# Second products of the mixture of experts in pairs: bursts of two experts on TensorE

## The chip, the cores and the metric

The kernel runs on one core of a Trainium2 chip. The core has TensorE (PE; its weight loads are listed as PEld), VectorE (DVE), ScalarE (ACT), GpSimd (POOL) and SyncE (SP), which only issues DMAs here. Each engine works through its own queue in order, and they meet at semaphores. The metric is the time of one execution on the device in microseconds; it is the median of several runs.

## What is computed

Four layers follow each other on x of 8 x 1024 x 256 floats: causal attention, a feed-forward layer with product-key experts, a rotary attention, and a mixture of experts. Only the last is touched by the change. Cut to what matters:

```python
x = x + mixture(layernorm(x))

def mixture(x):                     # D=256, H=8 slices, E=16 experts, K=2, HD=32, I=128
    h = x @ Wm + bm
    t = h.reshape(tokens * H, HD)   # each token has 8 slices of 32 numbers
    w = softmax(t @ expert_emb)     # 16 gates for each slice
    topw, topi = top_k(w, K)
    hmid = gelu(einsum('td,edi->tei', t, W1) + b1)
    eo = einsum('tei,eio->teo', hmid, W2) + b2
    comb = sum(eo[topi] * topw)     # the two chosen experts
    return comb.reshape(tokens, D) @ Wo + bo
```

The kernel works out all 16 experts for every slice and multiplies by a gate that is zero for those not chosen.

## The kernel before

`mixture_ffn` (from line 1942) is the stage. It cuts the tokens into NM = 16 blocks of TM = 512. A block has NU = 32 units: two halves hc of the features (4 slices each) by E = 16 experts. Tokens lie along the free dimension, 512 at a time.

**A unit** u goes through five steps on four engines.
- `hidden` (PE, L2139): the first product, in two pairs p = 0, 1. A pair fills one of HPB = 3 buffers `hidden` in PSUM, of two banks each, with two matmuls of 512 columns (a slice each). Pairs are numbered k = 2u + p within the block, and pair k waits until the gelu of pair k - 3 is done.
- gelu (ACT, L2239): one activation of 128 x 1024 for a pair, into one of four slots of `gelu_out`.
- `expert_out` (PE, L2149): the second product of the unit, 4 slices in 4 column groups of the array, as 8 matmuls in the trace, into the one bank `expert_out`.
- `gate_unit` (DVE, L2336): adds b2 and multiplies by the gates in `gates_spread`, into `gated` (two slots), or, for the first expert of a half, into `combined`.
- `sum_up` (POOL, L2221): adds `gated` to `combined`. At the start of a block the same queue adds the bias row to the block's x tiles (L2210).

**The order on PE** is written out by hand: `hidden(u)`, then `expert_out(u - 1)`, then a piece if the tables give one for that u. Unit 0 of a block waits, besides, for the slices (`slices_in`), and its first pair for the last hidden pair of the block before whose buffer it takes over.

**The front** is the preparation of the next block, cut into pieces and laid between units by `FRONT_AT`: n (normalize two tiles, DVE), x (turn a tile, PE, then a DVE copy), h (project on Wm, PE, then two DVE operations), s (split for the two-part product, DVE), l (gate logits, PE, then a copy), m (maxima, DVE), d (logits less the maximum, and the mask, DVE), the exp on ACT (`EXP_AT`), r (sum and reciprocal, DVE), k (keep the two chosen, DVE, L2307), w (weigh, DVE, L2312), g (turn the gates, PE, L2116, then a copy). `OUTPUT_AT` lays the four outputs of the block before (L2124, with wo) at u = 15, 15, 16 and 17. All PE pieces use the one bank `misc_bank`: each waits (`misc_free`) until DVE has emptied it of the piece before.

**SP** stores the turned gates to DRAM (L2047) and spreads them from there over the partitions, four units at a time (L2057); it also stores and loads the slices of the next block. ACT issues the store of a finished block's output at u = 20.

**POOL's fences**: `let_front_pass` holds an addition back until the DVE piece that lies at the same place (n, s, d, k or w) is done.

Of the kernel before, what the change touches and what calls it, by code (L numbers as in the profile page):

```python
# [1941 lines left out]
def mixture_ffn(nc, X, STATS, MEAN, RS, B, weights, out, ident):  # L1942
# [10 lines left out]
    HPB = 3  # L1953
    GE, GGROUPS = 4, 4
    NG = NU // GE
    with ExitStack() as ctx:
# [3 lines left out]
        def sem(name):  # L1960
# [11 lines left out]
        LS = sb("logits", [P, TT, H, E])  # L1972
        LM = sb("logits_less_max", [P, TT, H, E])
        EX = sb("gate_exp", [P, TT, H, E])
        MK = sb("gate_mask", [P, TT, H, E])
# [8 lines left out]
        OP = ctx.enter_context(nc.psum_tensor("expert_out", [P, TM], F32))  # L1984
        MB = ctx.enter_context(nc.psum_tensor("misc_bank", [P, TM], F32))
# [12 lines left out]
        misc_done = sem("misc_done")  # L1998
        misc_free = sem("misc_free")
        lm_ready = sem("lm_ready")  # L2000
        ex_ready = sem("ex_ready")
        gates_kept = sem("gates_kept")
# [3 lines left out]
        o_done = sem("o_done")  # L2006
        y_ready = sem("y_ready")
# [5 lines left out]

        FRONT = [("n", 0), ("n", 1), ("x", 0), ("x", 1), ("x", 2), ("x", 3), ("h", 0), ("s", 0), ("h", 1), ("s", 1),
                 ("l", 0), ("m", 0), ("m", 1), ("d", 0), ("r", 0), ("k", 0), ("w", 0), ("g", 0)]
        ON_PE = "xhlg"
# [6 lines left out]
        FPB = TT + HC + 2  # L2023

        def before(m):

            return FPB if m == 0 else (FPB + TT) * m + FPB - TT

# [3 lines left out]
        def _(sp):  # L2032
# [12 lines left out]
            def store_gates(m, par):  # L2045
                sp.wait_ge(misc_free, before(m) + 1)
                sp.dma_start(gate_d[par], GTS[:, :]).then_inc(gates_stored, 16)  # L2047
                sp.wait_ge(gates_stored, 16 * (m + 1))

            def spread(m, par, q):  # L2050

                hc, e = divmod(GE * q, E)
                if m or q >= GGROUPS:
                    sp.wait_ge(y_ready, NU * m + GE * (q - GGROUPS + 1) + 1)
# [26 lines left out]
            for t in range(TT):  # L2081
                sp.wait_ge(misc_free, before(NM - 1) + TT + t + 2)
# [4 lines left out]
        def _(pe):  # L2087
            pe.sem_inc(o_done, 2)

            def turn_x(m, t, k):  # L2090
                pe.wait_ge(xn_ready, TT * m + t + 1)
                pe.wait_ge(misc_free, k + 1)
                for c in range(DC):
                    mm = nc.tensor.transpose(MB[:, c * P:(c + 1) * P], XN[:, t, c * P:(c + 1) * P], ident[:, :])  # L2094
                mm.then_inc(misc_done, 1)

            def project(m, h, k):
                pe.wait_ge(misc_free, k + 1)
                for c in range(DC):
                    mm = nc.tensor.matmul(MB[:, :], wm[:, c, h * P:(h + 1) * P], XT[:, c, :],  # L2100
                                          start=(c == 0), stop=(c == DC - 1))
                mm.then_inc(misc_done, 1)

            def logits(m, _, k):
                pe.wait_ge(misc_free, k + 1)
                for t in range(TT):
                    for h in range(HC):
                        mm = nc.tensor.matmul(MB[:, t * P + h * G * E:t * P + (h + 1) * G * E],  # L2108
                                              HX[:, h, t * P:(t + 1) * P], embd[:, :, :], start=True, stop=True)
                mm.then_inc(misc_done, 1)  # L2110

            def turn_gates(m, _, k):
                pe.wait_ge(gates_ready, m + 1)
                pe.wait_ge(misc_free, k + 1)
                for t in range(TT):
                    mm = nc.tensor.transpose(MB[:, t * P:(t + 1) * P], EXP[:, t, :], ident[:, :])  # L2116
                mm.then_inc(misc_done, 1)

            def output(m, par, t, k):
                if t == 0:  # L2120
                    pe.wait_ge(y_added, NU * m + NU + 1)
                pe.wait_ge(misc_free, k + 1)
                for h in range(HC):
                    mm = nc.tensor.matmul(MB[:, 0:D], CM[:, par, h, t * P:(t + 1) * P], wo[:, h, :],  # L2124
                                          start=(h == 0), stop=(h == HC - 1))
                mm.then_inc(misc_done, 1)

            def hidden(m, par, u, first):

                hc, e = divmod(u, E)  # L2130
                for p in range(2):
                    k = 2 * u + p
                    if k >= HPB:
                        pe.wait_ge(gelu_done, NP * m + k - HPB + 1)
                    elif not first:
                        held = next(i for i in range(NP - 1, 0, -1) if i % HPB == k)
                        pe.wait_ge(gelu_done, NP * m - NP + held + 1)
                    for j in range(2):
                        mm = nc.tensor.matmul(HP[k % HPB][:, j, :], w1s[:, e, :], HS[:, par, G * hc + 2 * p + j, :],  # L2139
                                              start=True, stop=True)  # L2140
                    mm.then_inc(a_done, 1)

            def expert_out(m, u):
                hc, e = divmod(u, E)
                n = NU * m + u
                pe.wait_ge(y_ready, n + 1)
                pe.wait_ge(gelu_done, 2 * n + 2)
                for j in range(G):
                    mm = nc.tensor.matmul(OP[HD * j:HD * (j + 1), :], w2[:, e, :],  # L2149
                                          GH[:, (2 * u + j // 2) % 4, j % 2, :], start=True, stop=True,  # L2150
                                          tile_position=(0, HD * j))
                mm.then_inc(o_done, 1)

            front = {"x": turn_x, "h": project, "l": logits, "g": turn_gates}

            def one_block(m, par, first, last):
                k = before(m)
                for u in range(NU):
                    if u % E == 0:
                        pe.wait_ge(slices_in[u // E], 16 * 4 * (m + 1))  # L2160
                    hidden(m, par, u, first)
                    if u >= 1:
                        expert_out(m, u - 1)
                    elif not first:
                        expert_out(m - 1, NU - 1)
                    for t in () if first else OUTPUT_AT.get(u, ()):
                        output(m - 1, 1 - par, t, k)
                        k += 1
                    if u in FRONT_AT and FRONT_AT[u][0] in ON_PE and not last:
                        part, t = FRONT_AT[u]  # L2170
                        front[part](m + 1, t, k)
                        k += 1
                return k

            k = 0
            for part, t in FRONT:
                if part in ON_PE:
                    front[part](0, t, k)
                    k += 1
            for m in range(NM):  # L2180
                k = one_block(m, m % 2, m == 0, m == NM - 1)
            expert_out(NM - 1, NU - 1)
            for t in range(TT):
                output(NM - 1, 1, t, k + t)

        @block.gpsimd
        def _(pool):
            pool.sem_inc(y_added, 1)

            def let_front_pass(m, u):  # L2190

                m, u = (m, u + 1) if u + 1 < NU else (m + 1, 0)
                if m >= NM - 1 or u not in FRONT_AT:
                    return
                part, t = FRONT_AT[u]
                if part == "n":
                    pool.wait_ge(xn_ready, TT * (m + 1) + 2 * t + 2)
                elif part == "s":
                    pool.wait_ge(slices_ready, HC * (m + 1) + t + 1)
                elif part == "d":  # L2200
                    pool.wait_ge(lm_ready, m + 2)
                elif part == "k":
                    pool.wait_ge(gates_kept, m + 2)
                elif part == "w":
                    pool.wait_ge(gates_ready, m + 2)

            def sum_up(m, par):
# [4 lines left out]
                for u in range(NU):  # L2212
                    hc, e = divmod(u, E)
                    n = NU * m + u
                    pool.wait_ge(y_ready, n + 2)
# [3 lines left out]
                    else:  # L2219
                        let_front_pass(m, u)  # L2220
# [7 lines left out]
        def _(act):  # L2228
            def gate_exp(m):
                act.wait_ge(lm_ready, m + 1)  # L2230
                nc.scalar.activation(EX[:, :, :, :], LM[:, :, :, :], ACT.Exp).then_inc(ex_ready, 1)  # L2231

            def one_block(m, first, last):
                for u in range(NU):
                    for p in range(2):
                        k = 2 * u + p
                        act.wait_ge(a_done, NP * m + k + 1)
                        act.wait_ge(o_done, NU * m + u + 1)
                        nc.scalar.activation(GH[:, k % 4, :, :], HP[k % HPB][:, :, :], ACT.Gelu, bias=b1c[:, u % E:u % E + 1])\  # L2239
                           .then_inc(gelu_done, 1)  # L2240
                    if u == EXP_AT and not last:
                        gate_exp(m + 1)
                    if u == OUT_STORE_AT and not first:
# [192 lines left out]
```

## Time and profile before

| | us |
|---|---|
| median of 3 runs | 4373.39 (4366.82 to 4375.27) |
| profiled execution | 4367.08 |
| its span, first to last instruction | 4365.3 |
| mixture stage, from the first hidden matmul | from 3056.9 to the end |

| engine | busy us over the span | share |
|---|---|---|
| PE | 4077.7 | 93% |
| DVE | 2814.8 | 64% |
| ACT | 2660.3 | 61% |
| POOL | 1553.9 | 36% |

Mean granted clock of PE over the whole span: 0.970.

The shares are means over four layers. What counts for the change is the last 1310 us or so, where the page's slices show PE at nine tenths or more in nearly all of them and ACT at eight. How to read on: first the busy times of one block by stretch, then the chain of waits, which names at each moment the work that everything behind it depended on; then, where the chain stays on one engine, the starts of single instructions, since the matmuls overlap at their ends and only the distance from start to start is what PE spends on one.

### The profile page before, as it was taken

To read this page: it belongs to the slowest core of one execution; us is meant where nothing else is said; L and a number is where in the kernel's file an instruction comes from. 1 tells how busy PE (TensorE), PEld (TensorE's weight loads), DVE (VectorE), ACT (ScalarE), POOL (GpSimd) and SP (SyncE) were. 2 spreads that over 40 slices of the span, in tenths; PEclk is the share of its full clock that TensorE was granted. 3 is DMA by queue.
4 is the path that set the end of the run, shared out by engine and by line. 5 is a ranking of instruction groups with operands and counts; after the bars stand their busy time and mean duration, and the time that the engine had idled before them with its cause. 6 is when DMAs were issued, how large, how long until landed. Compare 5 with 4: busy or idle time off the path is not lost. (4 is left out here: it accounts for less than half of the span.)

```text
span 4365.3 us, 65491 instructions
## 1 busy us (share of the span) xinstructions
PE 4077.7 (93%) x23476; PEld 2382.0 (55%) x23476; DVE 2814.8 (64%) x5635; ACT 2660.3 (61%) x3262; POOL 1553.9 (36%) x1303
## 2 busy tenths in 40 slices
PE   7999899999996899999999989997899999999999
PEld 4444444444444778788787765554344444444443
DVE  6777777777665887878787844554455555554553
ACT  2555555555565554545455524443788889888888
POOL 3122122222223453534344411120445545545545
PEclk7999999999997999999999999999999999999999
DMA  7334234333413324232323230000767666676663
GB/s 179 87 87 102 65 88 101 87 87 80 105 29 105 84 58 114 61 106 69 97 77 90 85 76 1 1 1 23 166 152 162 141 161 161 140 161 153 148 162 90
DMA packets 205762, 429.97 MB, mean 98 GB/s; under 512 B 47585, under 2 KB 72561, under 8 KB 189057
## 3 DMA queue, kind: packets, MB, share of 16 engines
q1 hardware_dynamic: 193360, 411.56, 39.0%
q0 software_dynamic: 4160, 6.35, 0.7%
q10 hardware_dynamic: 7920, 7.87, 0.6%
q8 instruction: 191, 3.13, 0.3%
q14 instruction: 131, 1.07, 0.1%
HBM read 338.59 MB, written 87.03 MB: 98 GB/s over the span
## 5 line engine op out<-in xcount | busy, mean ns | idle before, releaser
L2239 ACT ACTIVATE gelu_out<-hidden,b_col 128x1024 f32<-128x1024 f32 x1024 | 1084.3, 1112 | 163.0 <-PE hidden L2139 162.3
L705 DVE TENSOR_REDUCE maxima<-front 128x1 f32<-128x512 f32 (+3 forms) x1280 | 738.9, 631 | 223.6 <-PE front L513 129.3
L2221 POOL TENSOR_TENSOR combined<-combined,gated 128x512 f32<-128x512 f32 x480 | 619.5, 1291 | 663.6 <-DVE gated L2336 454.9
L605 ACT ACTIVATE probsT<-scoresT 128x1024 f32<-128x1024 f32 (+3 forms) x768 | 584.6, 811 | 298.0 <-PE scoresT L541 293.6
L1168 POOL TENSOR_TENSOR pair_sums<-sims 128x1024 f32<-128x1024 f32 x256 | 483.3, 1905 | 668.3 <-DVEq L1300 412.5
L2336 DVE SCALAR_TENSOR_TENSOR gated<-expert_out,b_col,gates_spread 128x512 f32<-128x512 f32 x480 | 360.1, 750 | 500.2 <-PE expert_out L2149 294.4
L2139 PE MATMUL hidden<-slice_stack,w_stack 128*128 128x512 f32 x2048 | 626.4, 428 | 15.0 <-ACT gelu_out L2239 15.0
L2149 PE MATMUL expert_out<-gelu_out,w_sb 128*32 128x512 f32 x4096 | 547.0, 606 | 26.1 <-DVE gated L2336 13.5
L2139 PEld LDWEIGHTS hidden<-slice_stack,w_stack 128*128 128x128 f32 x2048 | 351.8, 189 | 370.8 <-ACT gelu_out L2239 281.8
L1096 PE MATMUL dense<-xnT,dense_weights 128*128 128x512 f32 x2304 | 536.3, 394 | 13.7 <-ACT silu_down L1202 9.7
L450 POOL TENSOR_SCALAR_AFFINE_SELECT probsT<-probsT 128x512 f32<-128x512 f32 x256 | 162.5, 635 | 1009.9 <-ACT probsT L605 1009.8
L1096 PEld LDWEIGHTS dense<-xnT,dense_weights 128*128 128x128 f32 x2304 | 434.3, 189 | 113.5 <-ACT silu_down L1202 10.6
L507 PE MATMUL front<-k_stack,q_stack 62*128 62x512 f32 (+3 forms) x1536 | 442.2, 434 | 44.1 <-ACT values L589 14.2
L507 PEld LDWEIGHTS front<-k_stack,q_stack 62*128 62x128 f32 x1536 | 219.8, 195 | 301.1 <-DVE maxima L705 183.7
L1223 ACT ACTIVATE pair_exp<-pair_sums,neg_max 128x1024 f32<-128x1024 f32 x256 | 282.7, 1117 | 144.6 <-DVE expert_weight L1330 141.3
L556 PE MATMUL pv<-probsT,values 128*32 128x512 f32 (+3 forms) x3072 | 341.2, 518 | 1.8 <-POOL probsT L450 1.0
L541 PE MATMUL scoresT<-q_stack,k_stack 64*128 64x512 f32 (+3 forms) x1536 | 312.1, 415 | 25.4 <-ACT probsT L605 22.5
L1319 DVE SCALAR_TENSOR_TENSOR pair_exp<-pair_sums,top_pairs,pair_exp 128x1024 f32<-128x1024 f32 x256 | 322.4, 1281 | 10.7 <-ACT pair_exp L1223 10.7
L1330 DVE SCALAR_TENSOR_TENSOR expert_weight<-pair_exp,recip_z,expert_weight 128x1024 f32<-128x1024 f32 x192 | 246.5, 1284 | 8.4
L1133 PE MATMUL dense<-up_sb,silu_down 128*128 128x256 f32 x1024 | 231.8, 379 | 5.1 <-DVE silu_down L1351 5.1
L1127 PE MATMUL dense<-wd_sb,hiddenT 128*128 128x256 f32 x1024 | 236.0, 384 | 0.0
L541 PEld LDWEIGHTS scoresT<-q_stack,k_stack 64*128 64x128 f32 x1536 | 153.1, 192 | 143.7 <-ACT probsT L605 82.3
(205 smaller groups left out, 5124.5 us busy)
## 6 DMA issues: line engine op xcount, KB each, us to landing
gates_spread<-gate_scratch SPq DMA_DIRECT2D x512, 256.0 KB, 4.8
dense_weights<-dense_scratch SPq DMA_DIRECT2D x384, 256.0 KB, 2.8
stack_scratch<-split_parts SPq DMA_DIRECT2D x192, 256.0 KB, 3.1
slice_stack<-slice_scratch SPq DMA_DIRECT2D x128, 256.0 KB, 7.8
q_stack<-stack_scratch SPq DMA_DIRECT2D x64, 384.0 KB, 6.2
k_stack<-stack_scratch SPq DMA_DIRECT2D x64, 384.0 KB, 9.4
slice_scratch<-slice_parts SPq DMA_DIRECT2D x32, 512.0 KB, 6.1
out_x<-x_tiles ACTq DMA_DIRECT2D x15, 512.0 KB, 5.0
```

Source lines behind the costliest of these rows:

```text
L507: mm = nc.tensor.matmul(F[k % 3][:, a * w:at], QS[rows, hf, q, qt * P:(qt + 1) * P], KS[rows, hf, q, kc * BANK:kc * BANK + w], start=True, ...
L541: mm = nc.tensor.matmul(bank[:, e, at:BANK], KS[rows, hf, q, kt * P:(kt + 1) * P], QS[rows, hf, q, c * BANK + at:(c + 1) * BANK], start=Tr ...
L556: mm = nc.tensor.matmul(PV[32 * j:32 * (j + 1), at:BANK], V[:, n % 2, kt, (G * g + j) * HV:(G * g + j) * HV + 32], PT[:, i % NPT, j, at:BA ...
L605: nc.scalar.activation(PT[:, i % NPT, 2 * pr:2 * pr + 2, at:BANK], ST[pr][:, :, at:BANK], ACT.Exp, scale=SCALE).then_inc(probs_ready, 1)
L705: nc.vector.tensor_reduce(dst, F[k % 3][:, 0:parts * w].rearrange("p (a k) -> p a k", a=parts), AX.X, ALU.max)\
L1096: mm = nc.tensor.matmul(bank[:, :], DW[:, u % SLOTS, a, c, :], XT[:, m % 2, b, c, :], start=(c + i == 0), stop=(c == DC - 1 and i == 2))
L1168: nc.gpsimd.tensor_tensor(A[:, h, :].rearrange("p (i j) -> p i j", i=NR), SM[:, m % 2, t, 0, h, 0:NR].unsqueeze(2).to_broadcast([P, NR, NK ...
L2139: mm = nc.tensor.matmul(HP[k % HPB][:, j, :], w1s[:, e, :], HS[:, par, G * hc + 2 * p + j, :], start=True, stop=True)
L2149: mm = nc.tensor.matmul(OP[HD * j:HD * (j + 1), :], w2[:, e, :], GH[:, (2 * u + j // 2) % 4, j % 2, :], start=True, stop=True, tile_positi ...
L2221: nc.gpsimd.tensor_tensor(CM[:, par, hc, :], CM[:, par, hc, :], Y[:, u % 2, :], ALU.add)\
L2239: nc.scalar.activation(GH[:, k % 4, :, :], HP[k % HPB][:, :, :], ACT.Gelu, bias=b1c[:, u % E:u % E + 1])\
L2336: nc.vector.scalar_tensor_tensor(out=Y[:, u % 2, :] if e else CM[:, par, hc, :], in0=OP[:, :], scalar=b2c[:, e:e + 1], in1=GS[:, q % GGROU ...
```

## The change

The stage's order is written in bursts. A burst b takes the units 2b and 2b + 1: first the PE pieces that the table gives for it, then the four hidden pairs of both units, then the second products of units 2b - 1 and 2b. DVE follows the same order: what the PE pieces need of it, then `gate_unit` of both units, then the pieces that are DVE's alone. The numbers b run through all blocks (ALL = 256 bursts), and so do the hidden pairs and their buffers.

The banks `expert_out` and `misc_bank` become `out_bank0` and `out_bank1`, used in turn by second products and pieces alike. The list `USES` numbers these uses in their order; use i waits until DVE has freed use i - 2. `gelu_out` has six slots (GHB) instead of four, and a gelu of unit n waits for the second product of unit n - 3. To make room, the gate work of DVE shares its tiles with `xn` and `xnT`, so that n is now made for the block after the next, in bursts 14 and 15; the maxima come in three parts. POOL's fence for k is gone.

In bursts of a block: x 0 to 3, h and s 4 and 5, l 6, m 6 to 8, d 9, exp behind burst 10, outputs 0 to 2 of the block before in burst 11, output 3 and r in 12, k and w in 13 (and the output's store), g at the head of 14.

```diff
+    GHB = 6
+    BU = NU // 2
+    ALL = NM * BU
...
-        GH = sb("gelu_out", [I, 4, 2, TM])
+        GH = sb("gelu_out", [I, GHB, 2, TM])
...
-        OP = ctx.enter_context(nc.psum_tensor("expert_out", [P, TM], F32))
-        MB = ctx.enter_context(nc.psum_tensor("misc_bank", [P, TM], F32))
+        OB = [ctx.enter_context(nc.psum_tensor(f"out_bank{i}", [P, TM], F32)) for i in range(2)]
...
-        FRONT_AT = dict(zip((0, 1, 2, 3, 4, 5, 6, 7, 8, 9, 10, 11, 12, 13, 18, 19, 20, 22), FRONT))
-        EXP_AT = 14
-        OUTPUT_AT = {15: (0, 1), 16: (2,), 17: (3,)}
-        OUT_STORE_AT = 20
+        FRONT_AT = {0: [("x", 0)], 1: [("x", 1)], 2: [("x", 2)], 3: [("x", 3)], 4: [("h", 0), ("s", 0)],
+                    5: [("h", 1), ("s", 1)], 6: [("l", 0), ("m", 0)], 7: [("m", 1)], 8: [("m", 2)], 9: [("d", 0)],
+                    11: [("o", 0), ("o", 1), ("o", 2)], 12: [("o", 3), ("r", 0)], 13: [("k", 0), ("w", 0)],
+                    14: [("g", 0), ("n", 0)], 15: [("n", 1)]}
+        EXP_AT = 10
+        OUT_STORE_AT = 13
...
+        def outs(b):
+            return [("e", n, 0) for n in (2 * b - 1, 2 * b) if 0 <= n < NM * NU]
...
+            def take(*use):
+
+                if USE[use] >= 2:
+                    pe.wait_ge(bank_free, USE[use] - 1)
+                return bank(*use)
...
+            def hidden(n, p):
+
+                m, (hc, e) = n // NU, divmod(n % NU, E)
+                if (e, p) == (0, 0):
+                    pe.wait_ge(slices_in[hc], 16 * 4 * (m + 1))
+                k = 2 * n + p
+                if k >= HPB:
+                    pe.wait_ge(gelu_done, k - HPB + 1)
...
+            def expert_out(n):
                 pe.wait_ge(gelu_done, 2 * n + 2)
+                ob = take("e", n, 0)
...
+            for b in range(ALL):
+                for part, m, t in fronts(b, True):
+                    front[part](m, t)
+                hidden(2 * b, 0)
+                hidden(2 * b, 1)
+                hidden(2 * b + 1, 0)
+                hidden(2 * b + 1, 1)
+                for _, n, _ in outs(b):
+                    expert_out(n)
...
+            def gelu(n, p):
+                k = 2 * n + p
+                act.wait_ge(a_done, k + 1)
+                if n >= GHB // 2:
+                    act.wait_ge(bank_done, USE["e", n - GHB // 2, 0] + 1)
...
+            for b in range(ALL):
+                for part, m, t in fronts(b, True):
+                    front[part](m, t)
+                for _, n, _ in outs(b):
+                    gate_unit(n)
+                for part, m, t in fronts(b, False):
+                    front[part](m, t)
```

`turn_gates` on PE still begins with its wait for `gates_ready`, which w sets on DVE, and `fronts(b, True)` gives the PE pieces of burst b.

## Rows read from the trace of the kernel before

**Rows 1.** Busy time by stretch, a middle block: us, busy (x instructions), granted clock, DMA share, GB/s.
```profile
3566.20:3647.10 80.90, 78.21 (x441) 33.89 (x437) 42.05 (x90) 70.99 (x68) 41.10 (x31) 1.00 0.66 154
```

**Rows 2.** Chain of waits, start us, us, what, in a steady stretch.
```profile
3603.87 1.13 PE hidden L2139 x4
3605.00 0.99 PE expert_out L2149 x8
```

**Rows 3.** Timeline of PE in narrow windows: start us, us, engine line op out<-in xcount.
```profile
3627.01 0.61 PE L2149 MATMUL expert_out<-gelu_out,w_sb 128*32 128x512 f32 x4
3627.55 0.50 PE L2139 MATMUL hidden<-slice_stack,w_stack 128*128 128x512 f32 x1
3627.88 0.63 PE L2139 MATMUL hidden<-slice_stack,w_stack 128*128 128x512 f32 x2
3628.35 0.39 PE L2139 MATMUL hidden<-slice_stack,w_stack 128*128 128x512 f32 x1
3628.68 0.62 PE L2149 MATMUL expert_out<-gelu_out,w_sb 128*32 128x512 f32 x1
```

**Rows 4.** Timeline, PE and POOL: groups behind a wait, an addition and the bias.
```profile
3592.24 1.13 PE L2124 MATMUL misc_bank<-wo_sb,combined 128*128 128x256 f32 x4 [0.58 <-DVE x_tiles L2324]
3628.52 1.28 POOL L2221 TENSOR_TENSOR combined<-combined,gated 128x512 f32<-128x512 f32 x1 [0.84 <-DVE gated L2336]
3635.62 2.38 POOL L2210 TENSOR_TENSOR x_tiles<-x_tiles,bo_rows 128x1024 f32<-128x1024 f32 x1
3639.19 1.06 PE L2149 MATMUL expert_out<-gelu_out,w_sb 128*32 128x512 f32 x8 [0.90 <-DVE gated L2336]
```

**Rows 5.** Timeline of ACT around the exp.
```profile
3589.20 1.28 ACT L2231 ACT_TABLE_LOAD   x1
3592.43 3.13 ACT L2239 ACTIVATE gelu_out<-hidden,b_col 128x1024 f32<-128x1024 f32 x3
```

**Rows 6.** Chain of waits, pieces between units, a hidden group behind one, l a block later.
```profile
3572.22 1.91 PE misc_bank L2100 x4
3578.20 1.93 PE misc_bank L2108 x16
3598.75 1.06 PE misc_bank L2124 x4
3642.55 0.37 PE misc_bank L2094 x2
3642.92 0.93 PE hidden L2139 x4
3659.08 1.93 PE misc_bank L2108 x16
```

**Rows 7.** Border of two blocks: chain of waits, then timelines of PE and ACT.
```profile
3629.33 1.11 ACT gelu_out L2239
...
3630.58 0.71 PE L2139 MATMUL hidden<-slice_stack,w_stack 128*128 128x512 f32 x2 [0.84 <-ACT gelu_out L2239]
...
3631.33 1.11 ACT L2239 ACTIVATE gelu_out<-hidden,b_col 128x1024 f32<-128x1024 f32 x1 [0.89 <-PE hidden L2139]
```

**Rows 8.** Timeline: a gated, and keep, weigh and g in the prologue.
```profile
3629.81 0.75 DVE L2336 SCALAR_TENSOR_TENSOR gated<-expert_out,b_col,gates_spread 128x512 f32<-128x512 f32 x1 [1.37 <-POOL combined L2221]
...
3054.65 0.69 DVE L2307 TENSOR_TENSOR gate_exp<-gate_exp,gate_mask 128x512 f32<-128x512 f32 x1 [0.21 <-issue]
3055.44 0.69 DVE L2312 TENSOR_TENSOR gates<-gate_exp,gate_recip 128x512 f32<-128x512 f32 x1
3056.18 1.12 PE L2116 MATMUL misc_bank<-ident,gates 128*128 128x128 f32 x4 [7.86 <-DVE gates L2312]
```

**Rows 9.** DMA issues of the page: out<-in, queue, op xcount, KB each, us to landing.
```profile
gates_spread<-gate_scratch SPq DMA_DIRECT2D x512, 256.0 KB, 4.8
```

**Rows 10.** End of the kernel: first output in the timeline, then a stretch of 2 us.
```profile
4354.06 1.13 PE L2124 MATMUL misc_bank<-wo_sb,combined 128*128 128x256 f32 x4 [2.21 <-POOL combined L2221]
...
4356.00:4358.00 2.00, 1.58 (x4) 0.75 (x3) 0.38 (x1) 0.00 (x0) 0.00 (x0) 0.52 0.19 66
```

More of the change, by code:

```diff
@@ L2125, in output @@
                                           start=(h == 0), stop=(h == HC - 1))
[L2126 to L2146, printed above, removed]
+                mm.then_inc(bank_done, 1)
+            def hidden(n, p):
[5 more added lines that the diff above has]
+                    pe.wait_ge(gelu_done, k - HPB + 1)
+                for j in range(2):
+                    mm = nc.tensor.matmul(HP[k % HPB][:, j, :], w1s[:, e, :], HS[:, m % 2, G * hc + 2 * p + j, :],
+                                          start=True, stop=True)
+                mm.then_inc(a_done, 1)
@@ L2151, in expert_out @@
                                           tile_position=(0, HD * j))
[L2152 to L2173, printed above, removed]
@@ L2175, in _ @@
-            k = 0
+                mm.then_inc(bank_done, 1)
+            front = {"x": turn_x, "h": project, "l": logits, "g": turn_gates, "o": output}
             for part, t in FRONT:
                 if part in ON_PE:
[L2178 to L2182, printed above, removed]
+                    front[part](0, t)
+            for b in range(ALL):
[7 more added lines that the diff above has]
+                    expert_out(n)
@@ L2183, in _ @@
+            for _, n, _ in outs(ALL):
+                expert_out(n)
             for t in range(TT):
-                output(NM - 1, 1, t, k + t)
+                output(NM - 1, t)
         @block.gpsimd
@@ L2230, in gate_exp @@
                 act.wait_ge(lm_ready, m + 1)
-                nc.scalar.activation(EX[:, :, :, :], LM[:, :, :, :], ACT.Exp).then_inc(ex_ready, 1)
-            def one_block(m, first, last):
-                for u in range(NU):
-                    for p in range(2):
[L2236 to L2243, printed above, removed]
-                        act.wait_ge(misc_free, before(m) + (0 if last else FPB - 1) + TT + 1)
-                        act.dma_start(tiles_out[:, TT * (m - 1):TT * m, :], X[:, TT * (m - 1):TT * m, :])\
-                           .then_inc(stored, 16)
@@ L2248, in _ @@
-            gate_exp(0)
-            for m in range(NM):
-                one_block(m, m == 0, m == NM - 1)
+                nc.scalar.activation(EX, LM, ACT.Exp).then_inc(ex_ready, 1)
+            def gelu(n, p):
[3 more added lines that the diff above has]
+                    act.wait_ge(bank_done, USE["e", n - GHB // 2, 0] + 1)
+                nc.scalar.activation(GH[:, k % GHB, :, :], HP[k % HPB][:, :, :], ACT.Gelu, bias=b1c[:, n % E:n % E + 1])\
+                   .then_inc(gelu_done, 1)
@@ new lines, in store_out @@
+            def store_out(m):
+                act.wait_ge(bank_free, USE["o", m, TT - 1] + 1)
+                act.dma_start(tiles_out[:, TT * m:TT * (m + 1), :], X[:, TT * m:TT * (m + 1), :]).then_inc(stored, 16)
+            gate_exp(0)
+            for b in range(ALL):
+                for n in (2 * b, 2 * b + 1):
+                    for p in range(2):
+                        gelu(n, p)
+                if b % BU == EXP_AT and b // BU + 1 < NM:
+                    gate_exp(b // BU + 1)
+                if b % BU == OUT_STORE_AT and b >= BU:
+                    store_out(b // BU - 1)
@@ L2277, in split, with logits, maxima @@
                   .then_inc(slices_ready, 1)
[L2279 to L2283 removed]
+            def logits(m, _):
+                ob = done("l", m, 0)
+                nc.vector.tensor_copy(flat(LS), ob[:, :].rearrange("p (g e) -> p g e", e=E)).then_inc(bank_free, 1)
+            def maxima(m, part):
                 dve.drain()
[L2285 to L2287 removed]
+                for g in range(*MAXIMA[part]):
+                    nc.vector.max(M8[:, g // H, g % H, :], LS[:, g // H, g % H, :])
@@ L2328, in gate_unit @@
+            def gate_unit(n):
+                m, u = divmod(n, NU)
                 hc, e = divmod(u, E)
[L2329 to L2330 removed]
                 q, i = divmod(u, GE)
+                ob = done("e", n, 0)
                 if i == 0:
```

220 lines of the change are left out of this document (100 added, 120 removed).

## The prediction, made before the changed kernel was run

> **What bounds the kernel now.** Only the mixture stage changes: 16 blocks of 512 tokens, 32 units (experts of a half) each, from 3056.9 us to the end. I read the stretches first. A middle block takes 80.88 us (the piece l starts at 3578.20 and again at 3659.08, [rows 6]), with PE busy for 78.21, ACT for 70.99 and DVE for 42.05 at a granted clock of 1.00 [rows 1]. The chain of waits then says who leads: in the steady part it stays on PE, with hidden (first product) and expert_out (second product) by turns, 1.13 + 0.99 = 2.12 us a unit [rows 2]. Single starts show where these go [rows 3]: expert_out to the first hidden matmul 0.54, first to second 0.33, then 0.235 each, last hidden to expert_out 0.33, the first four expert_out matmuls to the second four 0.45 (a group of eight takes 1.06, [rows 4], a four 0.61). So 2.12 is PE's own pace without a wait, and changing from one form of matmul to the other is dear: about 0.09 + 0.09 + 0.10 per unit over the plain pitches. ACT runs gelus that wait for nothing at 1.04 each or a little less (three in 3.13, [rows 5]), so about 2.05 a unit: close behind, but not the bound.
>
> The pieces laid between units (front of the next block, output of the last) cost PE their own length less some 0.2, as the hidden group behind them shrinks from 1.13 to 0.93 [rows 6]: x 0.37, so 0.17 net; h 1.91, so 1.71; l 1.93, so 1.79 (0.99 behind it); o 1.06, so 0.86; g has four short matmuls where x has two, so 0.4. A block has 4 x, 2 h, 1 l, 1 g, 4 o: 0.7 + 3.4 + 1.8 + 0.4 + 3.4 = 9.7. With 32 x 2.12 = 67.9 that is 77.6; the other 3.3 are stalls. One is at the border of blocks, where hidden 0 shares its bank with the last hidden pair and waits for its gelu: the previous expert_out began at 3628.68, the next hidden was due 0.45 + 0.54 later at 3629.67 and starts at 3630.58, 0.9 late [rows 3, 7]. Another 0.9 is an expert_out that waits for gated through POOL's bias addition, and the second output waits for the one misc bank: its idle is 0.58, behind a matmul that it would have overlapped by some 0.2, so it starts 0.8 late [rows 4]. The remaining 0.5 to 0.7 goes with the exp.
>
> **Bursts (the main term).** The new order on PE is: pieces, hidden pairs 4b, 4b+1, 4b+2, 4b+3, then expert_out 2b-1 and 2b. PE's own time falls: 0.33 + 6 x 0.235 + 0.33 + 3 x 0.45 + 0.54 = 3.96 a burst, where two units took 4.24: 0.28 saved. That expert_out follows expert_out at 0.45 isn't in the trace; its bounds are 0.43 and 0.54 (a change of form), and I take the row of the same form.
>
> But there are still three hidden buffers. Pair 4b+3 needs the one of pair 4b, so it waits for gelu 4b. Until now the wait was old by a unit when it was reached; now PE comes to it 0.33 + 5 x 0.235 = 1.50 after the burst's first matmul. Gelu 4b starts 0.75 after its hidden pair's start in the released case [rows 7], 0.77 with a second matmul at 0.33 in place of 0.31; it takes 1.11, and 0.14 later PE goes on [rows 7]. So pair 4b+3 starts at 2.02, not 1.50. After a wait its second matmul comes at 0.31 (0.71 for two, less the last one's 0.39 to 0.40) [rows 3, 7], expert_out 0.33 behind, at 2.66. Then 3 x 0.45 + 0.54 end the burst at 4.55. Is gelu 4b really started by PE and not held by ACT? Four gelus end at about 0.77 + 4 x 1.04 = 4.9, the next hidden is ready at 4.55 + 0.77 = 5.3: ACT stands idle and the loop closes on itself, at 4.55. Per burst that is 0.31 more than before, and 16 x 4.55 = 72.8 per block, 4.9 to 5.0 more. Expert_out 2b needs gelu 4b+1, done at about 0.77 + 1.01 + 1.11 + 0.14 = 3.03, and starts at 3.11: just covered; if that slips, PE waits there too. The six gelu slots free ACT of an old wait that the trace doesn't show as a cost: nothing.
>
> **Two banks and the pieces.** Each use waits for the use before the last. Gated starts 1.13 after its expert_out [rows 8] and takes 0.75: for 2b-1 that is 3.79 to 4.54, for 2b 4.70 to 5.45. The first piece behind a burst is due at 4.55 and gets its bank at about 4.6: 0.03 to 0.05 in ten bursts, 0.3 to 0.4 a block. Three outputs in a row find theirs (due at 5.55, free at 5.5; due at 6.4, free at 6.3), so the 0.8 goes. The border wait goes (pairs are now counted through), and so does the bias wait: behind gated 31 POOL adds until about 6.0 and biases until 8.4, by 1.28 and 2.38 [rows 4], and the next gated that needs it comes at 9.4. The exp with its table loads takes 3.23 of ACT (3592.43 - 3589.20, [rows 5]); it now lies beside three outputs, 2.6 of PE, and ACT's spare 0.5: 0.1 left. So all 3.3 of stalls go, 0.4 come.
>
> **The gates' turn (the second term).** keep and weigh now stand in burst 13 behind its two gated, and PE's turn g is the first thing of burst 14, ahead of its hidden pairs. Before, a unit lay between them (weigh at u 20, g at u 22). In the prologue keep, weigh and g follow each other without cover: 3054.65, 3055.44, 3056.18, so 1.53 from keep to g [rows 8]. Here keep can start at 5.45 + 0.09 = 5.54, g at 7.07, and PE was due at 4.6: a stall of 2.5 in each of 15 blocks. All hidden pairs of burst 14 are queued behind that wait, and ACT, out of input, with them. Keep also lost its fence against POOL's addition; bounds 2.2 and 3.0. SP's store and spread of the gates follow g later than before: g to the first gated of the next block is some 14 us; copy, store and spread are under 1.5 + 2 x 4.8 = 11.1 (the store counted like a spread, [rows 9]). Covered by 3; if not, PE waits the difference.
>
> **PE's clock.** At the end of the kernel PE stood idle 2.21 before the first output, and the granted clock was 0.52 in 4356 to 4358, that is mostly 1.2 GHz [rows 10]. The stall of 2.5 is as long. How long a drop lasts I can't read here; if it is about as long again as the stall or a little more, PE loses about half of that, less what the wait for gelu 4b hides anyway: 1.2, an estimate. I count 8 drops in 15 stalls, 10 us; bounds 0 and 25.
>
> The Trainium skill (TensorE: Matmul & The Clock Gate, section "A second HAM failure mode: psum-queue depth-cycling") speaks against this change more widely: PE that micro-idles between groups of matmuls while it cycles through PSUM banks can lose its clock again and again. No row here shows that from waits of 0.5; the block's 1.00 with stalls of 0.9 in it speaks against. It is rival C.
>
> **The sum.** Middle block: 72.8 + 9.7 + 0.4 + 0.1 + 2.5 = 85.5, against 80.88: +4.6, times 14 = 64. Last block: no front and no g, +5.0 - 0.8 = +4. Block 0 has no outputs and waits for gates by DMA; +3.5, between 0 and 8. The clock +10. Prologue and last outputs gain from the second bank, by the 0.8 of an output wait at some seven places: -6, between 0 and -10. Together +75. The profiled execution took 4367.08 (span 4365.3), 6.3 below the median of 4373.39. So 4442 for a profiled one, and 4448 as a median.
>
> **Rivals.** A: the sum, 4448. Its own range is 4405 (no clock loss, and 0.24 for a pair's second matmul after a wait, so 0.07 x 256 = 18 less, and more from the ends) to 4495 (expert_out to expert_out at 0.54, +23; clock +25). B: g's stall is covered by something I miss: 37 less and no clock loss, 4401. C: PE's clock falls in the bursts as well. At half clock a burst's own PE time is about 7.5, 3.0 more than 4.55; were that so in a quarter of 256 bursts, +190: 4638. D, the other side: PE gets ahead, and gelu 4b is started by ACT's own pace, so pair 4b+3 finds its buffer free. Then PE's own time bounds: 16 x 3.96 + 9.7 + 0.4 + 2.5 = 76.0 a block, 4.9 less than before, 15 blocks -73, ends -6, clock +5: 4299. It decides at the point where PE's part after the wait plus 0.77 is shorter than ACT's three gelus left: counted from the end of gelu 4b, 0.14 + (4.55 - 2.02) + 0.77 = 3.44 against 3 x 1.04 = 3.12. The reserve is 0.3; two expert_out groups would have to be a sixth shorter than their rows. E: the bursts' change of forms saves more than two units' rows say and pays for the waits: within 0.2%.
>
> **How the numbers follow.** A 0.70, B 0.08, C 0.05, D 0.11, E 0.06. The range 4395 to 4495 holds A and B and nothing of the rest. A measurement of this kernel tells about 0.2% (9 us) from no change. Slower: A, B, C and a little of E, 0.84; same 0.05; faster 0.11.
>
> **What would show it.** Right: some 256 waits of the fourth hidden pair for gelu, 0.5 each; ACT idle 0.4 to 0.5 before the first gelu of each burst; hidden starts 4.55 apart from burst to burst in bursts 7 to 9; 15 waits of g for weigh of 2.5; no wait at block borders; blocks of 85 to 87. Wrong: the fourth pair at 1.50 without a wait (D), g without a wait (B), or a clock well under 1.00 in blocks' middles (C).

## The result and the profile after

The changed kernel takes 4437.6 us (median of 4 runs, 4421.06 to 4446.83) against 4370.1 for the kernel before (4 runs): slower by 67.5 us, a ratio of 1.0153 with a 95% interval of 1.0126 to 1.018. I had said 4448, and slower by 75.

The page first. The span has grown by 71.1 us, while no engine has over 1.3 us more to do: PE is busy for 4065.8 us (before 4077.7), ACT for 2633.9 (2660.3), DVE for 2816.1 (2814.8). What was added is idle time. The columns are busy us, share of the span and instructions, then the costliest group with the idle time before it.

```profile
span 4436.4 us, 65528 instructions
...
PE 4065.8 (92%) x23476; PEld 2414.1 (54%) x23476; DVE 2816.1 (63%) x5635; ACT 2633.9 (59%) x3262; POOL 1555.0 (35%) x1303
...
L2239 ACT ACTIVATE gelu_out<-hidden,b_col 128x1024 f32<-128x1024 f32 x1024 | 1057.5, 1115 | 260.7 <-PE hidden L2158 260.5
```

One middle block, by stretch (same columns as [rows 1]); the granted clock is 1.00 as before. Below it the starts of the piece l in two blocks that follow each other, from the chain of waits: a block is now 85.25 us long.

```profile
3666.20:3751.40 85.20, 77.17 (x439) 35.57 (x437) 42.05 (x91) 69.24 (x68) 41.10 (x32) 1.00 0.64 145
...
3697.70 1.97 PE out_bank L2129 x16
3782.94 1.97 PE out_bank L2129 x16
```

Who waits for whom, from 3100 to 4400 us (us in total, times, longest); the last two rows are of the kernel before, from 3100 to 4300. The third row has no forerunner there.

```profile
ACT gelu_out L2239 <- PE hidden L2158: 239.1, 230, 4.7
PE hidden L2158 <- ACT gelu_out L2239: 72.0, 242, 3.2
PE out_bank L2137 <- DVE gates L2316: 40.5, 15, 3.0
...
ACT gelu_out L2239 <- PE hidden L2139: 140.1, 158, 1.8
PE hidden L2139 <- ACT gelu_out L2239: 15.0, 16, 2.3
```

PE waits 242 times for a gelu in front of a hidden pair, where before it did so 16 times, about once a block. ACT waits 230 times for PE, 239 us in all, where before it was 158 times and 140 us. Each now waits for the other about once a burst. And 15 times, once a block that has a front, the turn of the gates waits for w on DVE, 2.7 us each. (The row of 242 shows only 0.3 us each. In the trace a matmul lasts 0.39 to 0.40 us, though the next can start 0.235 after it, so the first 0.16 of a wait count as busy.)

The chain of waits in a burst without a piece (start us, us, what); [rows 2] and [rows 7] are what answers to it before.

```profile
3617.87 0.68 PE hidden L2158 x2
3618.55 0.02 issue
3618.57 1.12 ACT gelu_out L2239
3619.69 0.04 issue
3619.74 0.73 PE hidden L2158 x2
3620.47 1.85 PE out_bank L2166 x16
3622.33 0.68 PE hidden L2158 x2
```

Before, the chain stayed on PE here. Now it leaves PE in every burst for one whole gelu. The timeline of PE for the same burst gives the starts:

```profile
3617.80 1.67 PE L2158 MATMUL hidden<-slice_stack,w_stack 128*128 128x512 f32 x6
3619.74 0.73 PE L2158 MATMUL hidden<-slice_stack,w_stack 128*128 128x512 f32 x2 [0.27 <-ACT gelu_out L2239]
3620.40 1.92 PE L2166 MATMUL out_bank<-gelu_out,w_sb 128*32 128x512 f32 x16
3622.26 0.97 PE L2158 MATMUL hidden<-slice_stack,w_stack 128*128 128x512 f32 x3
```

The fourth pair starts 1.94 after the first, the burst ends at 4.46; two units took 4.25.

The gates' turn, chain of waits:

```profile
3653.05 0.75 DVE gated L2340
...
3653.89 0.94 DVE xnT L2311
...
3654.91 0.70 DVE gates L2316
3655.61 0.04 issue
3655.66 1.12 PE out_bank L2137 x4
```

The second gated of burst 13, k (its output tile is a part of `xnT` now), w, and only then g; g is the next thing in PE's queue, so PE stands still. k takes 0.94 where it took 0.69 [rows 8], with an addition of POOL beside it. This is so in all 15 blocks (0.39 to 0.40 us of overlap with the addition); in the prologue of the changed kernel, with the same tiles and no addition beside it, k takes 0.69. So it is the company of POOL and not the new tile.

### The profile page after: what moved, and what is told of

It reads as the page before. It is cut to its first block and busy times, and to the rows that moved or that the text cites. A ratio compares the mean times of both kernels' runs of the same rounds, so it can differ in the third digit from the quotient of the medians.

```text
span 4436.4 us, 65528 instructions
## 1 busy us (share of the span) xinstructions
PE 4065.8 (92%) x23476; PEld 2414.1 (54%) x23476; DVE 2816.1 (63%) x5635; ACT 2633.9 (59%) x3262; POOL 1555.0 (35%) x1303
## 5 line engine op out<-in xcount | busy, mean ns | idle before, releaser
L2239 ACT ACTIVATE gelu_out<-hidden,b_col 128x1024 f32<-128x1024 f32 x1024 | 1057.5, 1115 | 260.7 <-PE hidden L2158 260.5
L2340 DVE SCALAR_TENSOR_TENSOR gated<-out_bank,b_col,gates_spread 128x512 f32<-128x512 f32 x480 | 360.2, 750 | 624.1 <-PE out_bank L2166 600.2
L2166 PE MATMUL out_bank<-gelu_out,w_sb 128*32 128x512 f32 x4096 | 496.0, 602 | 3.5 <-DVE combined L2340 3.0
L507 PE MATMUL front<-k_stack,q_stack 62*128 62x512 f32 (+3 forms) x1536 | 441.7, 434 | 46.3 <-ACT values L589 15.8
L2166 PEld LDWEIGHTS out_bank<-gelu_out,w_sb 128*32 128x32 f32 x4096 | 107.3, 109 | 253.4 <-issue 169.9
```

What stands on the lines that cost most here:

```text
L507: mm = nc.tensor.matmul(F[k % 3][:, a * w:at], QS[rows, hf, q, qt * P:(qt + 1) * P], KS[rows, hf, q, kc * BANK:kc * BANK + w], start=True, ...
L2166: mm = nc.tensor.matmul(ob[HD * j:HD * (j + 1), :], w2[:, n % E, :], GH[:, (2 * n + j // 2) % GHB, j % 2, :], start=True, stop=True, tile_ ...
L2239: nc.scalar.activation(GH[:, k % GHB, :, :], HP[k % HPB][:, :, :], ACT.Gelu, bias=b1c[:, n % E:n % E + 1])\
L2340: nc.vector.scalar_tensor_tensor(out=Y[:, u % 2, :] if e else CM[:, m % 2, hc, :], in0=ob[:, :], scalar=b2c[:, e:e + 1], in1=GS[:, q % GGR ...
```

## The experiments

**Theory A**: the loss has two sources, the wait of each burst's fourth hidden pair for its first gelu, and g's wait for w. Both lie on PE's path, and everything else in the change gains. **Rivals**: R1, g's wait only stands in front of the gates' way over DRAM; R2, bursts save what they should and the two shared banks or the pieces' places cost the time; R3, the changes between the two forms of matmul aren't what PE loses, so bursts have nothing to give; R4 is named with the last kernel. The runs were made on several chips, so between chips I compare ratios to the kernel before, or block lengths in the traces.

### The gates' two steps a burst earlier

```diff
-                    11: [("o", 0), ("o", 1), ("o", 2)], 12: [("o", 3), ("r", 0)], 13: [("k", 0), ("w", 0)],
+                    11: [("o", 0), ("o", 1), ("o", 2), ("r", 0)], 12: [("o", 3), ("k", 0), ("w", 0)],
```

> The changed kernel, with r one burst earlier (behind the outputs of burst 11) and k and w in burst 12, so that w is done a whole burst before g is due. Theory A (the loss has two sources, the fourth pair's wait for gelu 4b in 256 bursts, and g's wait for w in 15 blocks at 2.7 us each): only the second goes, -41 us, 4397; bursts without a piece stay at 4.46 us, burst 13 with g behind it falls from 7.6 to about 4.9. Rival R1 (g's wait stands in front of another that ends as late, the gates' way over DRAM to the next block's first unit): g's wait goes and the same 2.7 us come back at the block's border, 4438.

Measured: 4387.4 us, 1.0045 of before (1.003 to 1.006). Against the changed kernel's 4437.6 (another chip) that is 50 less; by the ratios it is 47. The rows of g waiting for w are gone; a middle block went from 85.25 to 82.65 us, the burst up to the one with g from 7.61 to 5.02, and nothing came back at the border. R1 falls. 15 x 2.6 are 39. Another 3 are half clock: in the changed kernel's trace it followed three of the 15 stalls of g (more on this below), here none. The rest I put down to the spread between runs and chips.

### The bursts alone undone

```diff
                 hidden(2 * b, 0)
                 hidden(2 * b, 1)
+                for _, n, _ in outs(b)[:-1]:
+                    expert_out(n)
                 hidden(2 * b + 1, 0)
                 hidden(2 * b + 1, 1)
-                for _, n, _ in outs(b):
-                    expert_out(n)
+                expert_out(2 * b)
```

> The changed kernel with the bursts alone undone: hidden pairs of unit 2b, second product 2b-1, hidden pairs of unit 2b+1, second product 2b; two banks, numbering, tables and g's place stay. Theory A: the wait for gelu 4b is out of the way, the changes of form come back; two units take 4.2 us and not 4.46, so 256 x 0.26 = -67 us, 4371. Rival R2 (bursts save what they should, and the loss lies in the two shared banks and the places of the pieces): two units get longer by the saved changes, 0.28 to 0.38 us, so +70 us or more, 4508.

Measured: 4380.2 us, 1.0017 of before (0.9997 to 1.0037). Two units take 4.25 us again for 4.46, in all bursts without a piece. R2 said slower than the changed kernel; it is faster by some 57. The block became only 3.3 us shorter though (81.9), where 16 x 0.21 = 3.4 and 1.2 at the pieces were to be had (the two kernels with early gates differ by 82.65 - 78.07 = 4.6). Here the clock falls to 0.50 at every one of the 15 stalls of g, from 0.4 before it starts to 0.8 behind. Three of them, each in a window behind g:

```profile
3558.00:3560.00 2.00, 2.00 (x7) 1.72 (x7) 0.69 (x1) 0.18 (x1) 1.20 (x1) 0.50 0.00 0
3640.00:3642.00 2.00, 2.00 (x8) 1.65 (x7) 0.69 (x1) 0.24 (x1) 1.13 (x1) 0.50 0.00 0
3722.00:3724.00 2.00, 2.00 (x8) 1.58 (x6) 0.69 (x1) 0.32 (x1) 1.06 (x1) 0.50 0.00 0
```

### Both

> Both edits of the two runs above. Theory A: the two sources add up, -41 - 67, 4330, below the kernel before by 40 us: what is left are the gains of two banks, counting through and the pieces' places (3.2 us a block were stalls). Rival R2: 4467. Rival R1: 4371.

Measured: 4323.0 us, 0.989 of before (0.9865 to 0.9916). Both sources gone, the kernel is faster than the one before by 45 us. So all that the change brought besides these two is, taken together, a gain of that size; its parts (two shared banks, pairs counted through, places of the pieces, six gelu slots) were not run one by one. A block takes 78.07 us; PE's own 67.9 and 9.7 are 77.6, so of the 3.3 of stalls before 0.5 are left. The chain of waits of this kernel no longer leaves PE:

```profile
3616.36 0.93 PE hidden L2158 x4
3617.29 0.99 PE out_bank L2166 x8
3618.29 1.13 PE hidden L2158 x4
3619.42 0.99 PE out_bank L2166 x8
```

### The pieces in the gap

The bursts stay (r, k and w are early); the PE pieces move from the head of the burst to between its third and fourth pair.

```diff
-                for part, m, t in fronts(b, True):
-                    front[part](m, t)
                 hidden(2 * b, 0)
                 hidden(2 * b, 1)
                 hidden(2 * b + 1, 0)
+                for part, m, t in fronts(b, True):
+                    front[part](m, t)
                 hidden(2 * b + 1, 1)
```

> The changed kernel with r, k and w a burst earlier, and the PE pieces of a burst laid between its third and its fourth hidden pair, where PE waits for gelu 4b. Theory A: in the ten bursts with pieces the piece covers the wait of 0.4 us (x only 0.33 of it) and the bank's wait of 0.15 goes as well: about 5 us a block less than with r, k and w early alone, -75 us against it, 4325. If the fourth pair's wait is not on the path (rival R2): no gain, 4397.

Measured: 4330.5 us, 0.9918 of before (0.9891 to 0.9946); 57 less than with the pieces at the head, on the same chip. Two bursts of this kernel, without a piece and with g, in PE's timeline:

```profile
3596.82 1.67 PE L2158 MATMUL hidden<-slice_stack,w_stack 128*128 128x512 f32 x6
3598.76 0.73 PE L2158 MATMUL hidden<-slice_stack,w_stack 128*128 128x512 f32 x2 [0.27 <-ACT gelu_out L2239]
3599.42 1.92 PE L2166 MATMUL out_bank<-gelu_out,w_sb 128*32 128x512 f32 x16
3601.28 1.66 PE L2158 MATMUL hidden<-slice_stack,w_stack 128*128 128x512 f32 x6
3602.78 0.60 PE L2137 MATMUL out_bank<-ident,gates 128*128 128x128 f32 x4
3603.21 0.72 PE L2158 MATMUL hidden<-slice_stack,w_stack 128*128 128x512 f32 x2
3603.86 1.92 PE L2166 MATMUL out_bank<-gelu_out,w_sb 128*32 128x512 f32 x16
3605.72 1.67 PE L2158 MATMUL hidden<-slice_stack,w_stack 128*128 128x512 f32 x6
```

With g in the gap the fourth pair follows 1.93 after the first, without it 1.94: the piece costs nothing, since the wait was there anyway. I had 75 for this and it gave 57: the block is 3.8 shorter, not 5. Burst by burst, an x gave 0.33, which is all that it costs at the head with its bank's wait in it (1.3 in all where I had 1.9), and l, the last output and g together 2.4 where I had 1.7. But the two h gave only 0.3 where I had 1.1, and the burst with three outputs became 0.3 longer where I had it 0.5 shorter. Why the h and the outputs came short wasn't tried.

### The wait longer by a gelu

```diff
-                    pe.wait_ge(gelu_done, k - HPB + 1)
+                    pe.wait_ge(gelu_done, k - HPB + 2)
```

> The changed kernel with the wait of each hidden pair one gelu stricter (pair k waits for gelu k-2 where it waited for k-3), as if there were two buffers. Theory A: the fourth pair now starts behind gelu 4b+1, that is at 0.77 + 1.01 + 1.11 + 0.05 = 2.94 us after the burst's start and not at 1.94, and all behind it moves with it: a burst without a piece goes from 4.46 to 5.46 us, +256 us in all, 4694. Rival R2 (the buffer wait lies beside ACT's and DVE's own work, the banks set the pace): a burst grows by less than 0.5, below 4566.

Measured: 4692.3 us (one run; the kernel before 4372.4). The bursts without a piece take 5.46 us.

```profile
3617.16 1.20 PE L2158 MATMUL hidden<-slice_stack,w_stack 128*128 128x512 f32 x4
3619.10 0.74 PE L2158 MATMUL hidden<-slice_stack,w_stack 128*128 128x512 f32 x2 [0.74 <-ACT gelu_out L2239]
3620.10 0.73 PE L2158 MATMUL hidden<-slice_stack,w_stack 128*128 128x512 f32 x2 [0.27 <-ACT gelu_out L2239]
3620.76 1.92 PE L2166 MATMUL out_bank<-gelu_out,w_sb 128*32 128x512 f32 x16
3622.62 1.20 PE L2158 MATMUL hidden<-slice_stack,w_stack 128*128 128x512 f32 x4
```

The fourth pair comes at 2.94, the next burst at 5.46. Each microsecond of this wait is a microsecond of the burst; nothing lies beside it. That settles R2 from the other side. (A middle block without half clock grew by 15.8 us, for 16 bursts. At 12 of this run's 15 stalls of g the clock fell to half, which is in the total.)

### Bursts and units with short gelus

To see what bursts would give if the buffer came free in time, both orders (r, k and w early) with a gelu of half the length. The second slice of each pair gets no gelu of its own, and both second products read the first one's: that part of the computation is left out, PE's work is all there.

```diff
-                nc.scalar.activation(GH[:, k % GHB, :, :], HP[k % HPB][:, :, :], ACT.Gelu, bias=b1c[:, n % E:n % E + 1])\
+                nc.scalar.activation(GH[:, k % GHB, 0, :], HP[k % HPB][:, 0, :], ACT.Gelu, bias=b1c[:, n % E:n % E + 1])\
...
-                                          GH[:, (2 * n + j // 2) % GHB, j % 2, :], start=True, stop=True,
+                                          GH[:, (2 * n + j // 2) % GHB, 0, :], start=True, stop=True,
```

> Bursts with r, k and w early, with gelu on the first slice of each pair only (128 x 512), whose result both second products of the pair read; so the second slice's gelu is left out and the output isn't the reference's. PE's work is the same, a gelu takes about 0.69 us for 1.11. Theory A (the saved changes of form are real, and only the buffer's release outweighs them): the fourth pair finds its buffer free at 0.77 + 0.69 + 0.05 = 1.51 us, where PE comes to it anyway; a burst without a piece takes 4.03 us for 4.46, 256 x 0.43 = -110 us against the same kernel with whole gelus, 4277. Rival R3 (bursts save no changes of form worth naming): about 4.25 a burst as unit by unit, 4333.

> The same cut gelu in the order unit by unit with r, k and w early; the second slice's gelu is left out here too. Theory A: this order has no wait for gelu on its path, PE's own pace sets it: two units stay at 4.25 us, 4323 (to 4315, for ACT no longer late behind pieces). Then bursts with short gelus beat it by 40 to 50 us, which is what they save in changes of form. Rival (ACT's pace bounds the unit order too): it falls as the bursts do, to 4280 or below.

Measured, on one chip: bursts 4281.0 us (0.9809, 0.9793 to 0.9826), units 4317.0 us (0.9883, 0.9864 to 0.9903; a block takes 77.8 us, against 78.07 with whole gelus). Bursts without a piece take 4.03 us for 4.46, as expected to the hundredth, and pairs of units stay at 4.25. Here is such a burst, eight hidden matmuls in one row with no wait in them:

```profile
3619.35 2.24 PE L2158 MATMUL hidden<-slice_stack,w_stack 128*128 128x512 f32 x8
3620.12 2.42 ACT L2239 ACTIVATE gelu_out<-hidden,b_col 128x512 f32<-128x512 f32 x4 [1.61 <-PE hidden L2158]
3621.53 1.92 PE L2166 MATMUL out_bank<-gelu_out,w_sb 128*32 128x512 f32 x16
3623.38 0.95 PE L2158 MATMUL hidden<-slice_stack,w_stack 128*128 128x512 f32 x3
```

So the idea of the change is sound: fewer changes of form save 0.22 per two units without a piece. In all it is 36 us where I had 40 to 50. R3 falls. With whole gelus the release of the buffer takes 0.43 a burst and more than eats it.

### Three pairs at a time

As many pairs as there are buffers, then by turns two second products and one (the order of all engines follows from one list of such steps; r, k and w early).

```diff
+        def steps():
...
+            at, made = {-(-4 * b // 3): b for b in range(ALL)}, 0
+            for s in range(2 * NM * NU):
+                upto = min(NM * NU, 3 * (s // 2) + s % 2)
+                pairs = [k for k in range(3 * s, 3 * s + 3) if k < NM * NP]
+                yield at.get(s), pairs, [("e", n, 0) for n in range(made, upto)]
...
```

> With r, k and w early: steps of three hidden pairs, as many as there are buffers, then by turns two second products and one; so three units have two changes of form to and fro where single units have three and bursts 1.5, and no pair meets a buffer in use. Theory A: PE's own time is 3 units = 12 x 0.235 + 6 x 0.43 + 2 x (0.10 + 0.09 + 0.10) = 5.98 us, 1.99 a unit, close to ACT's 2.03, which then bounds the bursts without pieces; a block takes about 32 x 2.03 + 9.7 + 1 = 75.7 us against 78.1 of the unit order with early gates, so -38 us, 4285. If changes of form are not what PE loses (rival R3: PE waits anyway for what ACT and DVE return), the block stays at 78 or above, 4325.

Measured: 4314.2 us, 0.9868 of before (0.9837 to 0.9899): 58 us below the kernel before on its chip, but 29 above what I had expected. It has the lowest ratio of the kernels that compute everything, but its interval overlaps those of units with early gates (0.989) and of gap or units (0.9882), and its middle blocks take 76.6, 77.8 and 79.4 us by turns, 77.9 in the mean, where those take 78.07 and 77.92. So it can't be told from them. Three units without a piece take 6.47 us and not 6.1. PE's timeline says why my "no pair meets a buffer in use" was wrong:

```profile
3643.71 1.92 PE L2177 MATMUL out_bank<-gelu_out,w_sb 128*32 128x512 f32 x16
3645.57 1.67 PE L2169 MATMUL hidden<-slice_stack,w_stack 128*128 128x512 f32 x6
3647.17 1.07 PE L2177 MATMUL out_bank<-gelu_out,w_sb 128*32 128x512 f32 x8
3648.16 1.20 PE L2169 MATMUL hidden<-slice_stack,w_stack 128*128 128x512 f32 x4
3649.52 0.74 PE L2169 MATMUL hidden<-slice_stack,w_stack 128*128 128x512 f32 x2 [0.16 <-ACT gelu_out L2246]
3650.19 1.92 PE L2177 MATMUL out_bank<-gelu_out,w_sb 128*32 128x512 f32 x16
```

Behind the single second product the six hidden matmuls take 2.03 and not 1.60: the third pair of that step waits for the third gelu of the step before. PE comes to that pair 1.60 + 0.99 + 1.03 = 3.6 after the step before began; the third gelu is done after 0.77 + 3 x 1.01 + 0.1 + 0.05 = 3.95, and that is when the pair starts. The three buffers are the bound again, only later.

### Gap or units

A burst with a piece lays it in the gap, one without goes unit by unit (r, k and w early).

```diff
+                pieces = fronts(b, True)
...
+                if not pieces:
+                    for _, n, _ in outs(b)[:-1]:
+                        expert_out(n)
                 hidden(2 * b + 1, 0)
+                for part, m, t in pieces:
+                    front[part](m, t)
                 hidden(2 * b + 1, 1)
+                for _, n, _ in outs(b) if pieces else outs(b)[-1:]:
+                    expert_out(n)
```

> With r, k and w early: bursts that have a piece lay it before the fourth pair (the wait is covered), bursts without one go unit by unit (no wait). Theory A: the six bursts of a block without pieces go from 4.46 to 4.25 us, the others stay as with the pieces in the gap: 78.85 - 1.3 = 77.6 us a block, 4312. Rival R4 (the two orders disturb each other where they meet, since a unit order needs the second products one step earlier): 4330 or more.

Measured: 4320.8 us, 0.9882 of before (0.9854 to 0.991). A block takes 77.92 us for 78.85; the bursts without pieces 4.25, the one behind the exp 7.7 for 7.4. In that stretch the chain of waits stays on ACT, from 3660.3 us through the gelus and the exp to 3681.6, where PE goes on: the shorter bursts leave ACT no time to catch up. R4 falls, though the estimate was 9 us too good. Against units with early gates (0.989) it can't be told apart; their blocks are 78.07 and 77.92.

## Why the prediction was right

Step by step, with a middle block as the measure: 80.88 before, 85.5 said, 85.25 measured.

- **The burst.** Said 4.55, measured 4.46; 16 of them 71.4 for 72.8. The chain of reasoning held at each link: first pair to gelu 0.77, gelu 1.12, fourth pair behind it, ACT idle at each burst's start, the loop closed on itself. Two sizes were off. PE goes on 0.05 after a gelu that it waits for and not 0.14 as at the border in [rows 7], so the fourth pair starts at 1.94 instead of 2.02. And from the first expert_out matmul to the next burst it is 1.86 for 1.89. Both are small, but times 256 they make 23 us. One reading in the chain was wrong: expert_out 2b doesn't start at 3.11, that is the second half of 2b-1's group; by the sum's own steps it is 2.66 + 2 x 0.45 = 3.56. So it was covered by 0.5 and not just covered, and nothing in the sum hung on it.
- **The saved changes of form.** The half-length gelus show them: 4.25 - 4.03 = 0.22 a burst, where I had 0.28. In the trace of those bursts the fourth pair's second matmul still comes 0.34 after its first and not 0.235.
- **The gates' turn.** Said 2.5 with bounds of 2.2 and 3.0, measured 2.7. The difference is k's 0.94 for 0.69, the fence that I had named as a bound. Moving k and w made it go and nothing took its place.
- **The pieces.** Here I was too low. The four x cost 0.33 each and not 0.21, h, h and l together 5.6 for 5.3, the four outputs with the exp 3.9 for 3.6. The first piece's bank was to be late by 0.03 to 0.05; as the burst ends 0.09 earlier than I said, and 0.15 passes from gated's end to x's start, it is 0.2 late. Together about 1.1 us a block, and with g's 0.2 nearly what the shorter bursts gave back (1.4). That the block's total is closer than its terms is luck.
- **The stalls of before.** Border, bias and the second output went, as said. In the unit order with early gates 0.5 of 3.3 is left.
- **The clock.** Said 8 drops at 1.2 us, 10 in all. In the changed kernel the clock fell to 0.50 behind g in three of the 15 blocks: in block 0, and in two middle blocks, which are longer than 85.25 by 1.4 and 0.9. The two stretches below lie at g or just behind it in these two; the middle block by stretch above has the same stall of 2.7 us in it and stayed at 1.00.

```profile
3229.00:3231.00 2.00, 2.00 (x7) 1.62 (x6) 0.69 (x1) 0.60 (x1) 0.78 (x1) 0.50 0.00 0
3655.00:3657.00 2.00, 1.34 (x6) 1.25 (x7) 0.79 (x2) 0.00 (x0) 1.23 (x1) 0.51 0.00 0
```

So 10 us were counted and about 3 came. The price of one was right, the count was a guess. Rival C, the clock falling within the bursts, is out: 1.00 over a whole block, with a wait in every burst. The rule of the Trainium skill that I weighed (TensorE: Matmul & The Clock Gate, "A second HAM failure mode: psum-queue depth-cycling"), by which PE that micro-idles between groups of matmuls while it cycles through PSUM banks can lose its clock again and again, didn't show at waits of half a microsecond.
- **The ends.** Said -6 from prologue and last outputs. The last block with its end took 88.6 us for 87.7, where +4 for its bursts less 3 of these 6 were said. Of the 71.1 us between the profiled executions 67.2 lie behind the first hidden matmul. From the first turned tile to that matmul it took 22.9 for 24.5, but between 21.5 and 24.5 in the other kernels, whose prologue is the same as the changed one's, so the gain that I had counted there isn't shown. The first turned tile itself lies 5.4 us later, behind layers in which nothing was changed; between the other kernels' executions this start differs by more than that.

The middle blocks' 14 x 4.37 = 61, with 3.3 for block 0 (91.6 for 88.3, its half clock included), 2.2 for the clock in the middle blocks and 0.9 for the end make 67.6, and the trace has 67.2. That the medians differ by the same 67.5 is in part chance: the four runs of the changed kernel spread from 4421 to 4447. The forecast of 75 came as near as it did because its errors have both signs: bursts 23 too long, clock 7 too dear, pieces and g some 20 too cheap.

Rival D had its point of decision at 3.44 against 3.12, PE's part behind the wait against ACT's three gelus. Measured, the reserve was about as said: ACT was idle before the first gelu of every burst, 0.3 us in the bursts without a piece.

## What to carry to other kernels

Grouping like instructions to save changes of form lengthens the time between two uses of the same buffer; before counting the saving, walk once around the ring: first producer, consumer, release, and the producer that needs the buffer again. If that way is longer than the group, the engine can wait once per group, as here. Two remedies gained here over bursts with early gates: a smaller group (three pairs for three buffers, which still waited 0.3 us in every second step without a piece) and other work laid in front of the instruction that waits. Neither did measurably better than no groups at all. And a piece that another engine must finish first belongs a step away from it: the same k, w and g cost nothing or 2.7 us a block by their place alone.

## What was not expected of the hardware

- A stall of PE is followed by the half clock in some blocks or in all, and the stall's length doesn't decide it. In the changed kernel PE stood idle for 2.7 us at g and the clock fell in 3 of 15 blocks; with the same idle time and the wait longer by a gelu it fell in 12 of 15; with only the bursts undone PE stood idle for less, 2.4 us, and the clock fell in 15 of 15. The three kernels differ in the length of a block (85.25, 101 to 103 and 81.9 us); whether that decides it wasn't tried.
- What the two cost together: with the bursts undone, g's stall gone takes a block from 81.9 to 78.07, by 3.8 us. In block 0, where the clock fell only behind g, the burst up to g was 7.16 for 4.66, so the stall alone costs 2.5; the half clock then costs 1.3.
- PE goes on 0.05 us after the gelu that it waits for in a burst, where the border of blocks before had 0.14. Why the two differ wasn't tried.
- k on DVE took 0.94 us beside an addition of POOL and 0.69 without, and s 0.95 for 0.69.
